# Last cross attention of a decoder: which key tiles GpSimd adds, and behind which step it splits the next keys

## The chip, the cores and the metric

One core of a Trainium2 chip runs the whole kernel. The metric is the device time of one execution in microseconds. The kernel before took 2197.64 us, the median of three runs (2193.97 to 2198.96).

## The reference, cut to what matters

The program is a decoder of two layers on x (4 sequences of 256 rows, width 128) with a context of 4 x 1601 rows of width 64. Layer 0: complex attention, self attention plus cross attention, an expert layer with Sinkhorn routing. Layer 1: attention with rotary and Fourier terms, a block with a self attention and a cross attention, an expert layer. The change is in the cross attention of that last block (`a2`), which has 16 heads of width 32:

```
q = einsum('bsc,hcd->bhsd', xn, wq)
k = einsum('btc,hcd->bhtd', yn, wk)
v = einsum('btc,hcd->bhtd', yn, wv)
a = softmax(einsum('bhsd,bhtd->bhst', q, k) * D ** -0.5, axis=-1)
o = einsum('bhst,bhtd->bhsd', a, v)
```

with s over 256 queries and t over 1601 keys. The softmax subtracts each query's largest score and divides by the sum over all 1601 keys.

## The kernel before, in words

`stage_cross` (L1907) does this attention in NS = 16 groups s, one for each of four batches and four quarters of the heads; G = 4 heads stand in a group. The keys of a head are 13 tiles t of 128 (the last has 65), and a group takes them two at a time in STEPS = 7 steps p; step 6 has the last tile alone. Every engine runs its own list of instructions in order, written out by loops over (s, p); semaphores tie them together.

A group has two passes over the scores. The first finds the largest score of each query. TensorE multiplies bf16 parts of queries and keys (L2002, 32 matmuls of 401 columns for group s + 1, spread over the steps of group s by MAX_AT), VectorE takes maxima from PSUM (L2120), joins them (L2123) and writes them negated in two bf16 parts (L2128, L2131); TensorE turns these around into a row (L2023), in step 6. The keys for that pass come in three blocks of 32 rows in `kb`: the high bf16 part, the low part, the high part again. GpSimd splits the float32 keys `k32` of a group into `kh` (L2198, cast) and `kl` (L2200, subtraction); this is `halves(s + 2)`, called in group s. SyncE copies them into `kb` with twelve DMAs of 100 KB (L2246): four wait for the cast, eight for the subtraction. The first score matmul of group s + 2 stands in step 0 of group s + 1, behind that step's transposed scores, and waits for all twelve and for twelve copies of queries (L2239).

The second pass makes transposed scores tile by tile (L2038 and L2042 into PSUM banks 2 to 5), ScalarE takes the exponential of both tiles of a step at once (L2146) into `prob`, one of three buffers, and TensorE multiplies it with the values (`values`, L2055). The denominators are sums over the keys, made by matmuls with a matrix of ones (`ones`). For a step p in ADDED, GpSimd first adds the step's two tiles (`add`, L2215) into one of two buffers `both` (they are tiles with other names, `yT` and `z`, in the profile), and TensorE needs one set of 4 matmuls on the sum (L2076), done one step later. For a step not in ADDED, TensorE runs one set for each tile (L2069), without GpSimd. A float32 matmul is two instructions in the profile, so L2076 has 8 a sum and L2069 16 a step of two tiles.

In a step p TensorE does, in this order: transposed scores of p, three scores for the maxima, `values` of p - 1, the rest of the step's scores (in step 6 the shift matmul L2023), `ones` of p - 1, and then key or value matmuls of later groups. In even groups these are the keys of groups s + 2 and s + 3 in steps 0 to 3 (taken from PSUM by ScalarE, L2157), in odd groups the values. So `halves(s + 2)` waits in even groups for the last key chunk, made at the end of step 3; in odd groups its keys have been there since the group before.

GpSimd's list in a group is: add of step p where p is in ADDED, the division of the last group in step 1 (L2206), and `halves(s + 2)` behind the add of step 2. Before, ADDED = (0, 1, 2, 4, 5). `add` waits for the step's exponential and for TensorE to have read the buffer two sums back. The exponential waits for the add three steps back, whose `prob` buffer it overwrites.

Of the kernel before, what the change touches and what calls it, by code (L numbers as in the profile page):

```python
# [1809 lines left out]

STEPS = 7
MAX_AT = ((0, 5), (5, 10), (10, 15), (15, 20), (20, 26), (26, 32), (32, 32))
ADDED = (0, 1, 2, 4, 5)
CHUNKS = ((0, 401), (401, 400), (801, 400), (1201, 400))


# [90 lines left out]
def stage_cross(nc, k, name, scale, cT, wk, wv, srcT, wq, q, qh, ql, both, out):  # L1907


    NS = B * 4  # L1910
# [13 lines left out]
    def tiles_of(p):  # L1924
        return [t for t in (2 * p, 2 * p + 1) if t < KT_CTX]

    def sums_made(s, p):

        return s * len(ADDED) + sum(a <= p for a in ADDED)

    def batch(s):
        return s // 8 + 2 * (s % 2)

    def part(s):
        return s // 2 % 4
# [7 lines left out]
    with ExitStack() as ctx:  # L1943
# [21 lines left out]
        with nc.Block() as block:  # L1965
            @block.gpsimd
            def _(g_):
                g_.memset(negm[:, :, :, :], 0.0)
                g_.memset(onesb[:, :], 1.0)
# [5 lines left out]
        with nc.Block() as block:  # L1975
            @block.tensor
            def _(pe):
# [68 lines left out]
                def values(s, p):  # L2046
# [5 lines left out]
                    for t in tiles_of(p):  # L2052
                        rows = tile_rows(t)
                        for g in range(G):
                            ins = pe.matmul(k.ps[32 * g:32 * g + 32, 6, 0:N], vs[0:rows, s % 3, t, 32 * g:32 * g + 32],  # L2055
                                            prob[0:rows, n % 3, g, (t % 2) * N:(t % 2 + 1) * N],
                                            start=(t == 0), stop=(t == KT_CTX - 1), skip_group_check=True)
                    if p in ADDED and p - 1 not in ADDED:
                        ins.then_inc(probs_used.s, 1)

                def ones(s, p):
                    n = s * STEPS + p
                    if p in ADDED and p - 1 not in ADDED:
                        return
                    if p not in ADDED:
                        for t in tiles_of(p):
                            rows = tile_rows(t)
                            for g in range(G):
                                ins = pe.matmul(k.ps[32 * g:32 * g + 32, 6, N:2 * N], k.ones[0:rows, 0:32],  # L2069
                                                prob[0:rows, n % 3, g, (t % 2) * N:(t % 2 + 1) * N],  # L2070
                                                start=False, stop=(t == KT_CTX - 1), skip_group_check=True)
                    if p - 1 in ADDED:
                        m = sums_made(s, p - 1)
# [118 lines left out]
            @block.gpsimd  # L2192
            def _(g_):
                def halves(s):
                    g_.wait_ge(taken.s, taken.at(turns.made_at["key", s, 3] + 1))
                    if s > 0:
                        g_.wait_ge(ops[(s - 1) % 2].s, ops[(s - 1) % 2].at(16 * NDMA * ((s - 1) // 2 + 1)))
                    g_.tensor_copy(kh[:, :], k32[:, s % 4, :]).then_inc(split.s, 1)  # L2198
                    g_.wait_ge(split.s, split.at(2 * s + 1))
                    g_.tensor_tensor(kl[:, :], k32[:, s % 4, :], kh[:, :], ALU.subtract).then_inc(split.s, 1)  # L2200

                def divide(s):
                    g_.wait_ge(inverted.s, inverted.at(s + 1))
                    g_.wait_ge(out_read.s, out_read.at(s + 1))
                    o = (batch(s) * 4 + part(s)) * N
                    g_.tensor_tensor(out[:, o:o + N], sums[:, s % 2, 0:N], inv[:, s % 2, :],  # L2206
                                     ALU.mult).then_inc(divided.s, 1)

                def add(s, p):
                    n, m = s * STEPS + p, sums_made(s, p)  # L2210
                    g_.wait_ge(exp_done.s, exp_done.at(n + 1))
                    if m > 2:
                        older, at = divmod(m - 3, len(ADDED))
                        g_.wait_ge(probs_used.s, probs_used.at(older * STEPS + ADDED[at] + 2))
                    g_.tensor_tensor(both[m % 2].rearrange("p (g n) -> p g n", g=G), prob[:, n % 3, :, 0:N], prob[:, n % 3, :, N:2 * N],  # L2215
                                     ALU.add).then_inc(added.s, 1)

                for s in range(-2, NS):
                    for p in range(STEPS):
                        if s >= 0 and p in ADDED:  # L2220
                            add(s, p)
                        if p == 1 and s > 0:
                            divide(s - 1)
                        if p == 2 and s + 2 < NS:
                            halves(s + 2)
                divide(NS - 1)

# [860 lines left out]
```

## Time and profile before

| | |
|---|---|
| median of three runs | 2197.64 us |
| the profiled execution | 2193.25 us, span 2191.1 us |
| mean granted TensorE clock | 0.888 |
| TensorE busy in the span | 1736.3 us, 79% |
| VectorE, ScalarE, GpSimd busy | 1170.5, 960.0, 524.3 us |
| the stage in question | about 1478 to 1977 us of the span |
| transposed scores L2038 in it | 133.6 us of TensorE |
| denominators L2069, L2076 in it | 27.3 and 2 x 25.0 us of TensorE |
| adds L2215 on GpSimd | 2 x 94.2 us |

The profile shows one execution. Busy time of an engine that is not the last to arrive costs nothing, so the shares only say where to look; the timelines say who waits for whom. A line of a timeline has a start in us from the span's start, a length in us, an engine, and in square brackets how long the engine had been idle and what ended that. SPq is SyncE's queue of DMA issues; such a line lasts as long as the issue, not as the transfer. PEld is a weight load.

### The profile page before, as it was taken

The page shows a single profiled execution, that of the slowest core. Times are in us where ns is not written, and L with a number is a line of the kernel's source. Part 1 is how long each engine was busy: PE and PEld are TensorE (multiplying, and loading weights), DVE is VectorE, ACT ScalarE, POOL GpSimd, SP SyncE. Part 2 cuts the span into 40 slices and gives each one's busy share as a digit, 9 for nine tenths or more (in the row PEclk, how much of TensorE's full clock was granted, in tenths as well). Part 3 has the DMA queues.
Part 4 walks back from the last instruction along what each step waited for, and adds up shares of the span by engine and source line. Part 5 has one row for each costly group of instructions (what it writes and reads, how often), then busy time and mean ns, then how long its engine had stood idle before and what let it go on. Part 6 is the DMA issues. An engine that isn't in the chain of part 4 may idle for free. (4 is left out here: it accounts for less than half of the span.)

```text
span 2191.1 us, 43006 instructions
## 1 busy us (share of the span) xinstructions
PE 1736.3 (79%) x16607; PEld 952.5 (43%) x16607; DVE 1170.5 (53%) x2374; ACT 960.0 (44%) x1576; POOL 524.3 (24%) x392
## 2 busy tenths in 40 slices
PE   3684485899997259989899588469999999995698
PEld 1452352233334236654456255324444444444465
DVE  2573487888881336449542466355555555542312
ACT  1351253699994213211354235225555555552133
POOL 2011413000000000007444000115555555542000
PEclk8796697899999579989999779769999999998699
DMA  8423321222200220100000000031221122100000
GB/s 220 125 71 111 103 61 49 55 49 48 50 19 8 94 73 30 44 1 0 1 1 1 1 2 17 5 92 35 49 52 38 45 54 52 41 13 1 29 29 29
DMA packets 113050, 98.58 MB, mean 45 GB/s; under 512 B 21825, under 2 KB 97257, under 8 KB 112361
## 3 DMA queue, kind: packets, MB, share of 16 engines
q1 hardware_dynamic: 112872, 96.13, 16.6%
q8 instruction: 122, 2.00, 0.4%
q14 instruction: 56, 0.45, 0.1%
HBM read 54.44 MB, written 21.96 MB: 35 GB/s over the span
## 5 line engine op out<-in xcount | busy, mean ns | idle before, releaser
L2120 DVE TENSOR_REDUCE ta_mxp<-ps 128x1 f32<-128x401 f32 x512 | 262.2, 568 | 222.8 <-PE ps L2002 216.5
L1152 DVE TENSOR_REDUCE ac_mxp<-ps 128x2 f32<-128x802 f32 x256 | 241.3, 989 | 40.9 <-PE ps L1070 39.9
L2146 ACT ACTIVATE ta_prob<-ps 128x2048 f32<-128x2048 f32 (+1 forms) x112 | 196.5, 1755 | 127.2 <-PE ps L2042 127.2
L1181 ACT ACTIVATE cT<-ps 128x512 f32<-128x512 f32 (+1 forms) x416 | 225.9, 596 | 29.7 <-PE ps L1095 20.8
L2002 PE MATMUL ps<-ta_kb,ta_qb 96*128 96x401 bf16 x512 | 131.9, 352 | 11.2 <-DMA ta_qb<-qxl 11.2
L2038 PE MATMUL ps<-qxf,ta_k 32*128 32x256 f32 (+1 forms) x1664 | 133.6, 405 | 6.3 <-ACT ta_prob L2146 3.6
L1109 PE MATMUL ps<-cT 128*32 128x256 f32 (+1 forms) x1664 | 134.3, 394 | 0.5 <-ACT cT L1181 0.5
L2612 PE MATMUL ps<-xT,e_wi 128*128 128x512 f32 x256 | 116.0, 612 | 15.1 <-DMA e_wd<-in_e_down 10.3
L2215 POOL TENSOR_TENSOR yT<-ta_prob 128x1024 f32<-128x1024 f32 x40 | 94.2, 2354 | 115.1 <-ACT ta_prob L2146 94.4
L2622 PEld LDWEIGHTS ps<-e_wd,e_hid 128*128 128x128 f32 x1024 | 116.9, 192 | 7.7 <-issue 7.7
L2215 POOL TENSOR_TENSOR z<-ta_prob 128x1024 f32<-128x1024 f32 x40 | 94.2, 2355 | 103.9 <-ACT ta_prob L2146 83.6
L2622 PE MATMUL ps<-e_wd,e_hid 128*128 128x128 f32 x1024 | 116.9, 275 | 0.0
L2055 PE MATMUL ps<-ta_prob,ta_vs 128*32 128x256 f32 (+1 forms) x1664 | 113.0, 385 | 0.0
L1070 PE MATMUL ps<-ac_kb,ac_qz 50*128 50x401 bf16 x512 | 88.5, 352 | 25.5 <-DMA ac_qb<-qc 18.2
L2684 DVE SCALAR_TENSOR_TENSOR x<-ps,weight,x 128x128 f32<-128x128 f32 x128 | 36.0, 344 | 133.2 <-PE ps L2622 133.2
L2645 ACT ACTIVATE e_gate<-ps 128x512 f32<-128x512 f32 x64 | 38.2, 597 | 133.3 <-PE ps L2612 133.3
L1095 PE MATMUL ps<-ac_qb,ac_kb 50*128 50x256 bf16 (+1 forms) x832 | 83.0, 275 | 13.1 <-ACT cT L1181 7.5
L1339 POOL TENSOR_TENSOR o<-o,fenc 128x512 f32<-128x512 f32 x32 | 40.2, 1267 | 214.8 <-DVE o L1326 214.7
L2038 PEld LDWEIGHTS ps<-qxf,ta_k 32*128 32x128 f32 (+1 forms) x1664 | 65.8, 183 | 56.6 <-issue 38.1
L2002 PEld LDWEIGHTS ps<-ta_kb,ta_qb 96*128 96x128 bf16 x512 | 36.8, 98 | 106.7 <-DVE ta_mxp L2120 59.5
L2648 ACT ACTIVATE e_hid<-ps,e_b 128x512 f32<-128x512 f32 x64 | 44.0, 687 | 89.3 <-PE ps L2612 88.0
L2612 PEld LDWEIGHTS ps<-xT,e_wi 128*128 128x128 f32 x256 | 47.5, 196 | 77.8 <-issue 38.1
(323 smaller groups left out, 3343.6 us busy)
## 6 DMA issues: line engine op xcount, KB each, us to landing
ta_kb<-ta_kh SPq DMA_DIRECT2D x128, 100.1 KB
ac_kb<-kc SPq DMA_DIRECT2D x192, 50.0 KB
ta_kb<-ta_kl SPq DMA_DIRECT2D x64, 100.1 KB
v<-p_vt SPq DMA_DIRECT2D x16, 256.0 KB, 3.2
a_vs<-v SPq DMA_DIRECT2D x32, 128.0 KB, 2.6
e_wi<-in_e_in SPq DMA_DIRECT2D x8, 512.0 KB, 3.5
e_wd<-in_e_down SPq DMA_DIRECT2D x16, 256.0 KB, 3.7
kc<-c_part SPq DMA_DIRECT2D x12, 300.0 KB, 3.0
```

The costliest lines, as they stand in the source:

```text
L1070: ins = pe.matmul(k.ps[:, i % 2 * 2 + h, 0:401], qz[r, s % NBUF, gg, qt * P:(qt + 1) * P], kb[r, s % NBUF, gg, c * 400:c * 400 + 401], sta ...
L1109: ins = pe.matmul(k.ps[32 * g:32 * g + 32, 6, 0:N], vs[0:rows, s % 2, t, 32 * g:32 * g + 32], prob[0:rows, n % 3, g % 2, g // 2 * N:(g // ...
L1152: v.tensor_reduce(mxp[:, qt * G + 2 * gg:qt * G + 2 * gg + 2, c:c + 1], k.ps[:, i % 2 * 2:i % 2 * 2 + 2, 0:401], AX.X, ALU.max).then_inc(s ...
L1181: a.activation(prob[0:rows, n % 3, h, :], k.ps[0:rows, bank(("part", n, h)), :], ACT.Exp, scale=scale).then_inc(exp_done.s, 1)
L2002: pe.matmul(bank[:, 0:401], qb[:, s % 2, g, qt * P:(qt + 1) * P], kb[:, s % 2, g, c * 400:c * 400 + 401], start=True, stop=True).then_inc( ...
L2038: pe.matmul(k.ps[0:rows, 2 + g, (t % 2) * N:(t % 2 + 1) * N], k32[r, s % 4, t * P:t * P + rows], q[r, part(s), cols], start=True, stop=False)
L2055: ins = pe.matmul(k.ps[32 * g:32 * g + 32, 6, 0:N], vs[0:rows, s % 3, t, 32 * g:32 * g + 32], prob[0:rows, n % 3, g, (t % 2) * N:(t % 2 + ...
L2120: v.tensor_reduce(mxp[:, qt * G + g, c:c + 1], k.ps[:, turns.bank(slot), 0:401], AX.X, ALU.max).then_inc(scores_read.s, 1)
L2146: a.activation(prob[0:rows, n % 3, :, 0:w], k.ps[0:rows, 2:6, 0:w], ACT.Exp, scale=scale).then_inc(exp_done.s, 1)
L2215: g_.tensor_tensor(both[m % 2].rearrange("p (g n) -> p g n", g=G), prob[:, n % 3, :, 0:N], prob[:, n % 3, :, N:2 * N], ALU.add).then_inc(a ...
L2612: ins = pe.matmul(k.ps[:, 2 * n + u % 2, :], wi[:, par, n * F + f * P:n * F + (f + 1) * P], rhs, start=True, stop=True)
L2622: ins = pe.matmul(k.ps[:, 4 + c, t * P:(t + 1) * P], hid[:, f, (c * 4 + t) * P:(c * 4 + t + 1) * P], wd[:, par, f * C:(f + 1) * C], start= ...
```

## The change

Step 3 joins the steps whose two key tiles GpSimd adds, so that only step 6, which has one tile, is left out. The call that splits keys moves from behind the add of step 2 to behind the add of step 3. All loops that depend on ADDED follow: GpSimd has six adds a group instead of five; `ones` of step 3 has no L2069 matmuls and keeps the L2076 set for step 2's sum; `ones` of step 4, which had nothing to do, has the L2076 set for step 3's sum.

```diff
@@ -1810,7 +1810,7 @@
-ADDED = (0, 1, 2, 4, 5)
+ADDED = (0, 1, 2, 3, 4, 5)
@@ -2221,7 +2221,7 @@
                             add(s, p)
                         if p == 1 and s > 0:
                             divide(s - 1)
-                        if p == 2 and s + 2 < NS:
+                        if p == 3 and s + 2 < NS:
                             halves(s + 2)
                 divide(NS - 1)
```

## Rows read from the trace of the kernel before

**Rows 1.** Windows, 50 us of the stage: busy time of each engine, clock, DMA share.
```profile
core 0: us, PE busy (x) PEld busy (x) DVE busy (x) ACT busy (x) POOL busy (x), PEclk, DMA share, GB/s
...
1650.00:1700.00 50.00, 48.38 (x631) 22.45 (x634) 27.88 (x56) 27.23 (x29) 28.12 (x15) 1.00 0.19 43
```

**Rows 2.** Timeline of TensorE in group s = 5.
```profile
1653.34 0.64 PE L2076 MATMUL ps<-z,ones 128*32 128x256 f32 x8
...
1658.45 0.64 PE L2076 MATMUL ps<-yT,ones 128*32 128x256 f32 x8
...
1659.11 0.44 PE L2015 MATMUL ps<-wc,cT 64*65 64x128 f32 x4
...
1663.03 1.07 PE L2069 MATMUL ps<-ta_prob,ones 128*32 128x256 f32 x16
...
1664.46 0.71 PE L2038 MATMUL ps<-qxf,ta_k 32*128 32x256 f32 x8
...
1670.61 0.30 PE L2023 MATMUL ps<-identb,ta_negm 128*32 128x128 bf16 x8 [0.82 <-DVE ta_negm L2131]
```

**Rows 3.** Timeline of the last group, s = 15, between steps 4 and 5.
```profile
1969.45 2.35 POOL L2215 TENSOR_TENSOR yT<-ta_prob 128x1024 f32<-128x1024 f32 x1 [4.32 <-ACT ta_prob L2146]
1969.68 0.71 PE L2038 MATMUL ps<-qxf,ta_k 32*128 32x256 f32 x8
```

**Rows 4.** Groups by line: busy us, mean ns of one, idle before.
```profile
L2215 POOL TENSOR_TENSOR z<-ta_prob 128x1024 f32<-128x1024 f32 x40 | 94.2, 2355 | 103.9 <-ACT ta_prob L2146 83.6 <-PE ps L2076 20.4
...
L2069 PE MATMUL ps<-ta_prob,ones 128*32 128x256 f32 (+1 forms) x384 | 27.3, 386 | 0.0
L2076 PE MATMUL ps<-z,ones 128*32 128x256 f32 x320 | 25.0, 384 | 0.0
```

**Rows 5.** Timeline of GpSimd in group s = 5: add, then split.
```profile
1654.15 2.35 POOL L2215 TENSOR_TENSOR z<-ta_prob 128x1024 f32<-128x1024 f32 x1 [2.92 <-PE ps L2076]
1656.45 1.52 POOL L2198 CAST ta_kh<-ta_k 128x1601 bf16<-128x1601 f32 x1
1658.05 3.02 POOL L2200 TENSOR_TENSOR ta_kl<-ta_k,ta_kh 128x1601 bf16<-128x1601 f32 x1
```

**Rows 6.** Timeline of group s = 6: the block of step 3, then GpSimd.
```profile
1689.60 0.64 PE L2076 MATMUL ps<-z,ones 128*32 128x256 f32 x8
...
1691.77 1.52 POOL L2198 CAST ta_kh<-ta_k 128x1601 bf16<-128x1601 f32 x1 [3.90 <-ACT ta_k L2157]
...
1693.37 3.23 POOL L2200 TENSOR_TENSOR ta_kl<-ta_k,ta_kh 128x1601 bf16<-128x1601 f32 x1
...
1699.48 2.36 POOL L2215 TENSOR_TENSOR yT<-ta_prob 128x1024 f32<-128x1024 f32 x1 [0.56 <-ACT ta_prob L2146]
```

**Rows 7.** Waits of SyncE in the stage: us in total, times, longest.
```profile
SPq L2263 <- DMA ta_kb<-ta_kh: 1.6, 1, 1.6
```

**Rows 8.** Timeline of SyncE: last four key copies issued in s = 0, 1, 6.
```profile
1508.98 2.50 SPq L2246 DMA_DIRECT2D ta_kb<-ta_kh  x4
...
1536.62 3.68 SPq L2246 DMA_DIRECT2D ta_kb<-ta_kh  x4
...
1700.21 2.50 SPq L2246 DMA_DIRECT2D ta_kb<-ta_kh  x4
```

**Rows 9.** Timeline of TensorE: first scores on the keys of rows 8.
```profile
1514.04 0.69 PE L2002 MATMUL ps<-ta_kb,ta_qb 96*128 96x401 bf16 x3
...
1545.85 0.69 PE L2002 MATMUL ps<-ta_kb,ta_qb 96*128 96x401 bf16 x3
...
1704.48 0.67 PE L2002 MATMUL ps<-ta_kb,ta_qb 96*128 96x401 bf16 x3
```

**Rows 10.** L2128 of all groups (ns min/median/max), and its timeline in s = 6.
```profile
L2128 DVE SCALAR_TENSOR_TENSOR ta_negm<-ta_mx x16: 193/673/675, 1476.6 to 1950.8; 128x8 bf16<-128x8 f32 x16
...
1701.22 0.67 DVE L2128 SCALAR_TENSOR_TENSOR ta_negm<-ta_mx 128x8 bf16<-128x8 f32 x1
```

## The prediction

> **What bounds the kernel now.** I read the page first, then the windows of the last cross attention, its groups by line, the timelines of TensorE, GpSimd and SyncE through two of its sixteen groups (s = 5 and s = 6), and last the waits of SyncE. A group s is seven steps p; s = 0 to 13 also prepare keys for group s + 2.
>
> In the stage TensorE is busy 48.4 of 50 us at granted clock 1.00, VectorE 27.9, ScalarE 27.2, GpSimd 28.1 [rows 1]. So TensorE's instruction stream sets the pace, except for one idle place a group: before the shift matmuls of step 6 (L2023) it waits 0.82 us for VectorE's negated maxima [rows 2]. In the last group, which has no maxima left, ScalarE's exponentials set the pace instead [rows 3]. Three things lie close behind. GpSimd adds a pair of key tiles in 2.35 us [rows 4], and splits keys in 1.52 + 3.02 us [rows 5]. SyncE then copies the split keys in twelve DMAs, which the first score matmul of the next group needs. And VectorE's maxima chain has one instruction (L2128) that overlaps a GpSimd add.
>
> **What the change removes and adds on TensorE.** Before, step 3's denominators are 16 L2069 instructions, followed by the 8 of L2076 for step 2's sum. This block runs from 1663.03 to the next L2038 at 1664.46, so 1.43 us. A block of 8 L2076 alone takes from 1658.45 to 1659.11, 0.66 us [rows 2]. After, step 4 holds 8 L2076 (gain 1.43 - 0.66 = 0.77), and step 5, which had no such block, holds 8 (loss 0.66, at its end). By count of instructions, with a group's busy time over its count as the price: 256 fewer of L2069 at 27.3 / 384 = 71 ns are 18.2 us, 128 more of L2076 at 25.0 / 320 = 78 ns cost 10.0 [rows 4], 8.2 us for the stage. The two readings differ because of what follows: step 5's maxima are computed before its new block, so VectorE's chain starts 0.77 earlier, and the 0.66 falls into the 0.82 us for which TensorE now waits at L2023. If nothing else moved, each group with maxima would gain about 0.75 us: 15 such groups, 11.3 us. In the last group the exponential of step 4 is done at about 1969.43 (the add that waits for it starts at 1969.45) and TensorE comes at 1969.68, so 0.25 us is gained; the new block of step 5 hides under the next exponential. Ceiling: 11.5 us.
>
> **What it adds on GpSimd.** One add more a group, 2.35 us, in front of the split. It waits for two things: step 3's exponential, and the buffer that the denominators of step 2's block have read. Such an add starts 0.81 us after that block's start (1653.34 there, add at 1654.15; the block of step 3 is at 1658.45) and the cast after it 2.30 us after the add's start [rows 2, 5].
> Odd s (5): the cast would start at 1658.45 + 0.81 + 2.30 = 1661.56 instead of 1656.45, 5.1 us later.
> Even s (6): there the split already waits for the last key chunk until 1691.77; now 1689.60 + 0.81 + 2.30 = 1692.71, 0.95 us later [rows 6].
> The added wait blocks what is queued behind it on GpSimd: cast, subtraction, the adds of steps 4 and 5. Add 4 would end at about 1668.6 (odd) and 1699.9 (even). The block that needs it is in step 6, behind L2023 (1670.6 before), so there are 1 us and more to spare; the exponentials need adds three steps back, which is not near.
>
> **Where the split keys are needed.** SyncE waits for the cast (4 DMAs), then the subtraction (8 DMAs). When its last issue has ended the data isn't there yet: at the end of the stage SyncE itself waits 1.6 us from its last key issue to its landing [rows 7]. So a group's first score can start 1.65 us after the last key issue ended. (The Trainium skill, Perfetto Trace Analysis, section DMA Instruction — HWDGE, says that the record of the issue doesn't contain the movement; the trace agrees with its 1.6 us.)
> Even s: last issue ends at 1511.48 (s = 0) and 1702.71 (s = 6), ready 1513.13 and 1704.36; needed 1514.04 and 1704.48 [rows 8, 9]. That is 0.91 and 0.12 us of slack; over the seven even groups 0.9 on average, and 0.12 is the smallest.
> Odd s: 1540.30 (s = 1), ready 1541.95, needed 1545.85: 3.9 us; over the seven odd groups 4.3.
> The copies move with the split, so they cost 5.1 - 4.3 = +0.8 us per odd group, and 0.95 - 0.9 = +0.05 per even group (up to +0.8 in s = 6). None of the 0.75 gain is left in either, because the wait is counted from GpSimd's chain and not from TensorE's. TensorE stands at the score matmul in order, so values, denominators and the next scores queue behind it.
> Bounds of the copies: eight issues of 0.6 us and the landing, 6.5 us after the subtraction, when none is held up; many groups have one long issue (4 issues took 3.68 instead of 2.50 [rows 8]). The average of before is kept. Without long issues the slack needed shrinks by about 0.6 us per group (odd +0.2, even -0.5); if every group had one, +0.5.
>
> **The maxima chain.** L2128 reads two SBUF operands. It takes 0.67 us in 15 of 16 groups and 0.19 in the first, where GpSimd has nothing to do [rows 10]. In group 6 it runs 1701.22 to 1701.89, and the GpSimd add of step 5 from 1699.48 to 1701.84: it ends 0.05 us behind the add. I take it as held until that add ends. After the change adds 4 and 5 run back to back behind the split. Subtraction's end in even groups 1696.61 + 0.95 = 1697.56, plus 4.70: add 5 ends at 1702.26, 0.4 later than before (0.2 where the subtraction took 3.02 and not 3.23). In odd groups 1661.07 + 5.1 + 4.70 = 1670.9 against 1670.18, 0.7 later (0.9 with the longer subtraction). The next group's first score moves by the same, 0.2 to 0.4 and 0.7 to 0.9 us later.
> The Trainium skill says this as a rule (SBUF — State Buffer, section Who interferes with whom): a VectorE instruction with two SBUF inputs and a GpSimd instruction that reads SBUF exclude each other, the later one waits for all of the other. The rows agree so far, but they show no case in which the add ends at another distance; were the 0.67 a fixed price of overlap, this term would be nothing.
> Both delays end at the same matmul, so the larger counts: odd groups +0.9, even groups +0.4.
>
> **Sum.** 7 x 0.9 + 7 x 0.4 = 9.1; group 14 has no split and gains 0.75, group 15 gains 0.25. In all 9.1 - 1.0 = 8.1 us slower. The profiled execution took 2193.25 us (span 2191.1), 4.4 under the median of 2197.64; on it the sum gives 2201.3, on the median 2205.7. I forecast 2205.8.
>
> **Rivals.**
> 1. Copies only: L2128 isn't held longer. 7 x 0.8 + 7 x 0.05 - 1.0 = +5.0, 2202.6. For it: 0.67 us is the same in 15 groups. Against: its end follows the add's end.
> 2. Copies land in their shortest time, and L2128 slips in between adds 4 and 5 (in odd groups it is ready 0.0 to 0.2 us after add 4's end, a close thing). 7 x 0.2 - 7 x 0.5 - 1.0 = -3.1, with half of it +0; centre 2196.5, no change.
> 3. The other side: neither copies nor lock are late, and TensorE keeps 0.75 us in 15 groups: -11.5, 2186.1. It decides if the copies need under 5.7 us from the subtraction's end; none of before did, as eight issues alone take 4.9. Or the data comes before my 1.65 us says. Against: the slack of 0.12 us in group 6.
> 4. The delays add up, since the lock shifts the start of a group and long issues fall more often into the later copies: odd +1.7, even +0.7, 16.8 - 1.0 = +15.8, 2213.4.
>
> **How the numbers follow.** Forecast 0.40, rival 1 0.20, rival 2 0.15, rival 3 0.10, rival 4 0.15. No change is within 0.2% (4.4 us), about what a measurement of this kernel tells. Slower: forecast, rival 4 and most of rival 1, 0.71; same: rival 2 and a rest of rival 1, 0.18; faster: 0.11. The range leaves out rival 3 and the upper half of rival 4: 2196 to 2213. The likeliest case's own range is 2202 to 2210.
>
> **What would show it.** In the profile after: L2069 has 128 instructions in the stage, L2076 768, and L2215 96 adds. The cast in odd groups starts about 5.1 us later against step 3's block, in even groups 0.95. The first score of each of groups 1 to 14 has an idle time ahead of it ended by a DMA of ta_kb, up to about 1 us; or L2128 grows to about 1.5 to 2.2 us, with a longer wait at L2023. From the first score at 1514.04 to that at 1704.48 are six groups, 63.5 us for two of them [rows 9]; after, two take 64.8. Step 4 is 0.77 shorter and step 5 0.66 longer. I am wrong if the first scores wait for nothing and L2023's wait shrinks, or if two groups take under 63.5 us.

## The result, and the profile after

| | before | after |
|---|---|---|
| median | 2195.99 us (4 runs) | 2210.97 us (2210.13 to 2213.12, 4 runs) |
| ratio to before | | 1.0067, 95% interval 1.0053 to 1.0080 |
| profiled execution | 2193.25 us | 2211.78 us |
| its span, mean granted clock | 2191.1 us, 0.888 | 2209.7 us, 0.879 |

The kernel became slower by 15.0 us; 8.1 were forecast. The time lies within the stated range (2196 to 2213), but just outside the likeliest case's own 2202 to 2210. One execution among all runs, of **after_copies_first** below, took 2662.78 us at a granted clock of 0.625, and as it is the one that was profiled, that run is read by its other times alone.

The counts of the changed kernel's stage are as forecast (groups by line):

```profile
L2215 POOL TENSOR_TENSOR yT<-ta_prob 128x1024 f32<-128x1024 f32 x48 | 113.1, 2356 | 133.8 <-ACT ta_prob L2146 91.0 <-PE ps L2076 42.8
...
L2076 PE MATMUL ps<-z,ones 128*32 128x256 f32 x384 | 30.7, 392 | 0.0
...
L2128 DVE SCALAR_TENSOR_TENSOR ta_negm<-ta_mx 128x8 bf16<-128x8 f32 x15 | 29.7, 1979 | 0.5
...
L2069 PE MATMUL ps<-ta_prob,ones 65*32 65x256 f32 x128 | 10.6, 405 | 0.0
```

The third line is the finding: L2128 takes 1.98 us on average instead of 0.67 [rows 10]. The timeline of group s = 5 of the changed kernel, steps 4 to 6:

```profile
1666.73 0.71 PE L2038 MATMUL ps<-qxf,ta_k 32*128 32x256 f32 x8
...
1670.86 0.71 PE L2038 MATMUL ps<-qxf,ta_k 32*128 32x256 f32 x8
...
1673.39 2.36 POOL L2215 TENSOR_TENSOR yT<-ta_prob 128x1024 f32<-128x1024 f32 x1
...
1674.98 0.66 PE L2038 MATMUL ps<-qxf,ta_k 32*65 32x256 f32 x8
...
1675.70 2.35 POOL L2215 TENSOR_TENSOR z<-ta_prob 128x1024 f32<-128x1024 f32 x1
...
1675.96 2.15 DVE L2128 SCALAR_TENSOR_TENSOR ta_negm<-ta_mx 128x8 bf16<-128x8 f32 x1
1678.14 0.19 DVE L2131 SCALAR_TENSOR_TENSOR ta_negm<-ta_mx,ta_negm 128x8 bf16<-128x8 f32 x1
...
1678.49 0.30 PE L2023 MATMUL ps<-identb,ta_negm 128*32 128x128 bf16 x8 [1.73 <-DVE ta_negm L2131]
```

Each L2038 opens a step. Step 4 takes 4.13 us (4.99 before), step 5 4.12 (3.56 before). Adds 4 and 5 run back to back behind the split. L2128 starts 0.26 us after add 5 and ends at 1678.11, 0.06 behind it. TensorE idles 1.73 us before L2023, against 0.82 [rows 2].

The waits of TensorE in the changed stage, 1500 to 1970 us (us in total, times, longest):

```profile
PE ps L2023 <- DVE ta_negm L2131: 22.1, 14, 2.0
...
PE ps L2002 <- DMA ta_kb<-ta_kh: 0.9, 4, 0.3
```

In that window the first was 12.3 us before, 15 times, 0.8 at most. The second says that the key copies ended the wait of only 4 first scores, by 0.9 us together.

What comes next in that group is the other part. Windows of the changed kernel, before, at and after this idle time (the column after POOL is the granted clock):

```profile
1643.00:1676.00 33.00, 30.98 (x432) 15.56 (x432) 19.49 (x39) 17.52 (x20) 19.77 (x11) 1.00 0.21 48
1676.00:1679.70 3.70, 1.83 (x38) 0.84 (x34) 2.31 (x2) 1.20 (x2) 2.06 (x1) 1.00 0.69 161
1679.70:1689.90 10.20, 10.20 (x77) 4.18 (x73) 2.60 (x5) 3.74 (x6) 2.35 (x1) 0.50 0.09 22
1689.90:1700.00 10.10, 9.49 (x114) 4.03 (x107) 5.20 (x10) 5.55 (x6) 5.04 (x3) 1.00 0.01 2
```

TensorE is busy for 1.83 of 3.70 us, and then the clock stands at its lower level (1.2 GHz) for 10.2 us, with the engine busy throughout. The group that begins there, s = 6, took 36.6 us from its first L2038 to the next group's, about 4.5 more than its like. It happens a second time at 1747.9, for 3.4 us, behind a wait of 1.96 us at L2023 (s = 7), and costs about 1.4: 0.2 at the end of s = 7 and 1.2 in s = 8 (33.00 us, 31.80 in s = 4). Not each such wait brings a fall: s = 3 and 11 wait 1.95 us at the same place, and none followed. Before, the clock stayed at its upper level from 1487.2 us, within group 0, to the end of the last group.

Where the profiled difference of 18.5 us stands, by the starts of the same instructions in both traces: 5.2 us had come up before the stage (first L2038 at 1483.31 instead of 1478.10), in code the change doesn't touch, where the clock fell at other places; 13.3 us come in the stage; nothing after it. Of the 13.3, the two clock falls are some 5.9, the groups' own time some 7.4. The 5.2 us ahead of the stage are of these two executions: in the traces of all kernels here that ran at the usual clock, whose code ahead of the stage is the same, it starts anywhere from 1476.3 to 1484.2.

### The profile page after: what moved, and what is told of

Read it like the earlier page. It is cut to its first block and busy times, and to the rows that moved or that the text cites. A ratio compares the mean times of both kernels' runs of the same rounds, so it can differ in the third digit from the quotient of the medians.

```text
span 2209.7 us, 42782 instructions
## 1 busy us (share of the span) xinstructions
PE 1745.0 (79%) x16479; PEld 955.2 (43%) x16479; DVE 1191.6 (54%) x2374; ACT 960.2 (43%) x1576; POOL 560.9 (25%) x408
## 3 DMA queue, kind: packets, MB, share of 16 engines
q8 instruction: 121, 1.98, 0.4%
## 5 line engine op out<-in xcount | busy, mean ns | idle before, releaser
L2215 POOL TENSOR_TENSOR yT<-ta_prob 128x1024 f32<-128x1024 f32 x48 | 113.1, 2356 | 133.8 <-ACT ta_prob L2146 91.0
L2038 PE MATMUL ps<-qxf,ta_k 32*128 32x256 f32 (+1 forms) x1664 | 136.2, 411 | 6.2 <-ACT ta_prob L2146 3.7
L2215 POOL TENSOR_TENSOR z<-ta_prob 128x1024 f32<-128x1024 f32 x48 | 112.7, 2349 | 89.5 <-ACT ta_prob L2146 48.9
L2038 PEld LDWEIGHTS ps<-qxf,ta_k 32*128 32x128 f32 (+1 forms) x1664 | 67.0, 186 | 61.4 <-issue 43.0
L1044 POOL TENSOR_TENSOR oc<-ac_sums,ac_inv 128x256 f32<-128x256 f32 x16 | 11.7, 728 | 291.9 <-ACT ac_inv L1194 291.9
```

The source lines that it names most:

```text
L2038: pe.matmul(k.ps[0:rows, 2 + g, (t % 2) * N:(t % 2 + 1) * N], k32[r, s % 4, t * P:t * P + rows], q[r, part(s), cols], start=True, stop=False)
```

## Experiments

Times are medians, ratios are to the kernel before, timed on the same chip. The first four runs were timed on one chip, after_filled, max_in_psum_filled, odd_early_psum_copies and before_psum_copies on a second, and added_alone, after_copies_first and odd_only_psum_copies on a third; between these three sets the ratios are compared and not the times. A group's time is from its first L2038 (whatever its line is called there) to the next group's. Each edit stands on the kernel named in brackets; of an edit, the lines that matter are shown.

**max_in_psum** (on the kernel after) and **before_max_in_psum** (on the kernel before): the joined maxima go to eight unused columns of the last score's PSUM bank.

```diff
-                    v.tensor_reduce(mx[:, :], mxp[:, :, :], AX.X, ALU.max).then_inc(vec.s, 1)
+                    mx = k.ps[:, turns.bank(("max", s, 31)), 404:404 + 2 * G]
+                    v.tensor_reduce(mx, mxp[:, :, :], AX.X, ALU.max).then_inc(vec.s, 1)
...
-                    v.scalar_tensor_tensor(out=high, in0=mx[:, :], scalar=-2.0, in1=mx[:, :],
-                                           op0=ALU.mult, op1=ALU.add).then_inc(vec.s, 1)
+                    v.tensor_scalar(high, mx, -1.0, None, ALU.mult).then_inc(vec.s, 1)
...
-                    v.scalar_tensor_tensor(out=low, in0=mx[:, :], scalar=-1.0, in1=high,
+                    v.scalar_tensor_tensor(out=low, in0=mx, scalar=-1.0, in1=high,
```

> The changed kernel, with the joined maxima in PSUM, so that neither L2128 (now a negation of one operand) nor L2131 reads two SBUF operands. Theory 1 (the maxima chain is held by GpSimd's add of step 5): L2128 falls from 1.66 to 2.38 us to 0.2 though it still overlaps an add; step 6 of the groups loses 0.9 to 1.3 us, and part of it is taken by the key copies, which come next: the first scores now wait for a DMA. About 0.4 us a group, 6 us in all, and up to 5 more if the clock no longer falls inside the stage: 2200 to 2205. Theory 2 (the key copies alone set the groups' start, the long L2128 lies beside them): L2128 shrinks and nothing is gained, 2211. Theory 3 (0.48 us is a fixed price of overlap, not a lock): L2128 keeps a length over 0.6.

Measured: 2229.35 us, ratio 1.0138 (1.0115 to 1.0160). The time was missed by 24 us and more, the first half of the mechanism held. Timeline of its group 1, and its waits:

```profile
1550.64 2.38 POOL L2215 TENSOR_TENSOR z<-ta_prob 128x1024 f32<-128x1024 f32 x1
...
1550.89 0.20 DVE L2128 TENSOR_SCALAR ta_negm<-ps 128x8 bf16<-128x8 f32 x1
1551.12 0.19 DVE L2131 SCALAR_TENSOR_TENSOR ta_negm<-ps,ta_negm 128x8 bf16<-128x8 f32 x1
...
1551.50 0.29 PE L2022 MATMUL ps<-identb,ta_negm 128*32 128x128 bf16 x8
...
1555.19 0.68 PE L2001 MATMUL ps<-ta_kb,ta_qb 96*128 96x401 bf16 x3 [1.46 <-DMA ta_kb<-ta_kh]
```

```profile
PE ps L2001 <- DMA ta_kb<-ta_kh: 26.5, 14, 2.8
```

Both instructions take 0.2 us in the middle of a GpSimd add: the held time is gone. The changed opcode of L2128 isn't what did it: L2131 is the instruction it was, with one operand moved. Step 6 takes 2.43 us, where it took 3.9 to 4.8 in the changed kernel. Now all 14 first scores wait for the key copies, 26.5 us together, and the clock falls 11 times inside the stage, 74.9 us at its lower level. So the copies are the second limit, right behind the maxima chain, and idle time on TensorE costs more than its length: the full groups without a fall took 31.65 to 32.23 us, those with one 34.0 and more. This is the kernel that rival 1 had priced, with the copies alone, at 5.0 us over the kernel before; it came to 30 and more.

> The kernel before, with the joined maxima in PSUM. Theory 1: L2128 falls from 0.67 to 0.2 in 15 groups, the wait at L2023 from 0.82 to about 0.35, 0.48 us a group: 7 us faster than before, 2189. Theory 2: the wait at L2023 shrinks, but in the even groups the key copies, with their 0.9 us of slack, take over: some 5 us faster, 2191.

Measured: 2191.26 us, ratio 0.9976 (0.9961 to 0.9991). The two theories lay too close together to be told apart by the time, but only one first score waited for a copy (0.2 us); step 6 went from 3.44 to 2.96 us in each group.

**odd_split_early** (on the kernel after): the odd groups split behind step 2. **odd_early_max_in_psum**: the same with the maxima in PSUM.

```diff
-                        if p == 3 and s + 2 < NS:
+                        if p == (2 if s % 2 else 3) and s + 2 < NS:
```

> The changed kernel, but the odd groups split their keys behind the add of step 2, as before; the even groups behind that of step 3. Theory 1: in odd groups add 5 no longer queues behind the split, only behind TensorE's reading of its buffer at the end of step 5; L2128 ends some 0.1 us later than before the change, a group costs +0.14 instead of +0.8: 4.6 us less than the changed kernel, 2206, and up to 5 less again if the clock stays up. Theory 2 (copies): they leave at the old time in odd groups, so the same saving, but then the first scores of odd groups in the changed kernel must have waited for a DMA, which the trace shows in 4 places only.

Measured: 2198.09 us, ratio 1.0004 (0.9992 to 1.0016): no slower than before. Its group 5:

```profile
1666.31 0.64 PE L2076 MATMUL ps<-z,ones 128*32 128x256 f32 x8
...
1667.12 2.36 POOL L2215 TENSOR_TENSOR z<-ta_prob 128x1024 f32<-128x1024 f32 x1 [1.77 <-PE ps L2076]
...
1667.85 1.68 DVE L2128 SCALAR_TENSOR_TENSOR ta_negm<-ta_mx 128x8 bf16<-128x8 f32 x1
```

Add 5 here waits 1.77 us with GpSimd idle, for TensorE to read its buffer in the new block of step 5, and L2128 is held for it again. An odd group took 31.96 us, +0.15 over before, as expected (three took 0.3 more, with 0.2 to 0.3 us of it waiting for a copy); and no clock fall is left in the stage. The saving of 13 us in the medians is more than the 9.6 expected at most. In the traces the stage is 10.2 us shorter, 5.9 of it the clock's, so the steady part and the clock's part both lay in the odd groups' split; the rest is within the spread of what comes ahead of the stage.

> Both: odd groups split behind step 2, and the maxima chain free of the lock. Theory 1: odd groups and group 14 keep TensorE's gain, -0.7 us each, and the 0.48 of the lock of before; even groups are held by the key copies, -0.2. Together 7 us or more under the kernel before, 2189 or less. If the copies of the even groups cost more than that, 2193.

Measured: 2196.87 us, ratio 0.9997 (0.9982 to 1.0012): a miss. Even groups run in 30.35 us, and the next group's first score waits for their copies (10.0 us in 7 places), with four clock falls. One of the falls came behind an idle time of 1.1 us, while none came behind 1.95 us in the changed kernel's s = 3 and 11: the length of one idle time doesn't say whether the clock falls.

**after_filled** and **max_in_psum_filled**: matmuls without a reader ahead of a wait that stays. The edit of the first; the second puts three in front of the first score's wait.

```diff
+                        for _ in range(0 if s == 0 else 2 + (s + 1) % 2):
+                            pe.matmul(bank[:, 0:400], wk[half(s), part(s) * P:(part(s) + 1) * P],
+                                      cT[half(s), at_batch(s):at_batch(s) + 400], start=True, stop=True)
                         pe.wait_ge(negmax.s, negmax.at(s + 1))
```

> The changed kernel, with matmuls whose result nobody reads in front of the wait for the negated maxima in step 6 (two of 400 columns in even groups, three in odd ones, 0.47 us each, inside an idle time of 1.2 to 2.1 us). If part of the changed kernel's time is the granted clock that falls after these idle times: no fall inside the stage, some 3 to 5 us less, 2206 to 2208. If the falls are chance or don't matter: 2211 or a little more.

Measured: 2207.65 us, ratio 1.0049 (1.0029 to 1.0068). The trace has no clock fall in the stage; odd groups take 32.84 us and even ones 32.01, +1.0 and +0.35 over before. The added matmuls were priced too low: they are float32 and so two instructions each, two of them take 1.61 us and three 2.28, more than the waits that they stand in, and cost up to 0.4 us a group. The interval overlaps that of the change, so the median alone doesn't show the clock's share.

> max_in_psum with three such matmuls (1.4 us) in front of a group's first score, where that kernel waits 1.9 us on average for the key copies. Clock theory: the falls inside the stage (11 in its trace) go, the groups take 31.7 to 32.2 us as its undisturbed ones do, 2197 to 2201 instead of 2229. If the time of max_in_psum comes from the copies themselves being slower, it stays near 2229.

Measured: 2211.97 us, ratio 1.0066 (1.0046 to 1.0086). The three matmuls of group 2:

```profile
1543.62 2.28 PE L2000 MATMUL ps<-cT,wc 64*128 64x400 f32 x6
```

By the ratios, more work on TensorE made the kernel 16 us faster, and one clock fall is left of 11 (10.2 us at the lower level instead of 74.9). 14 times 2.3 us of added work are more than the 25 us of waiting that they replace, so the gain comes from the clock: this shows its share. The time stayed 11 us over what I expected: most groups took 32.6 to 32.8 us, since the filling takes 2.3 us and not the 1.4 that I had priced, and an undisturbed group waits 1.1 to 1.7.

**odd_early_psum_copies** (on odd_early_max_in_psum), **before_psum_copies**, **after_copies_first** (on the kernel after): eight of the twelve key copies issued before the subtraction's.

```diff
-                    for k_part, n, count in ((kh, 0, 1), (kl, 1, 2), (kh, 2, 2)):
+                    for k_part, n, count in ((kh, 0, 1), (kh, 2, 1), (kl, 1, 2)):
```

> odd_early_max_in_psum, with the second copy of the high key parts issued before the low part's, so that eight of twelve copies go out during the subtraction and only four stand behind it. Copies then land some 0.8 us earlier. If the copies are what ends the wait of the even groups (7 waits, 10.0 us in its trace) and with it what makes the clock fall: waits under 1 us, few falls, groups near 30.4 to 31 us, 2180 to 2186. If the queue of copies is bound by their data and not by their order: no gain, 2197.

Measured: 2189.83 us, ratio 0.9954 (0.9935 to 0.9973). By the ratios this is 9 us faster than odd_early_max_in_psum, but over the 2180 to 2186 expected: seven first scores still wait, 7.3 us in all, up to 1.3, and one clock fall is left of four.

> before_max_in_psum with the same order of copies. There only one first score waited for a DMA: under 1 us gained, 2190 to 2191. Were it faster by more, the copies would bound it in a way that the trace doesn't show.

Measured: 2187.93 us, ratio 0.9949 (0.9929 to 0.9968). The interval overlaps that of before_max_in_psum, and in the traces the stage is 0.6 us shorter, as expected.

> The changed kernel with the second copy of the high key parts issued before the low part's: all copies land some 0.8 us earlier, the maxima chain is as in the changed kernel. Lock theory: only what the first scores waited for (0.9 us in 4 places) can go, 2210, within noise of 2211. Copies theory: 0.8 us in each of 7 to 14 groups, 2200 to 2205.

Measured: 2212.58 us, ratio 1.0068 (1.0050 to 1.0087), the changed kernel's time. Earlier copies alone give nothing back, so they are not what makes the change slow.

**added_alone** (on the kernel before): only ADDED is changed.

> Half of the change: GpSimd adds the tiles of step 3 as well, but the split stays behind the add of step 2 in all groups. In odd groups this is odd_split_early: +0.14 us each. In even groups the split waits for the last key chunk with adds 3, 4 and 5 behind it; add 3 ends near the end of step 5, where TensorE wants it (up to 1 us late), add 5 would end 1.8 us later than before. Lock theory: even groups +0.3 (L2128 slips in between two adds) to +1.8, so 2198 to 2210, and in no case under the kernel before. If only the copies mattered, both kinds of group would have them as early as before, and the kernel would be some 8 us faster than before, 2189.

Measured: 2217.90 us, ratio 1.0106 (1.0080 to 1.0132), slower than the whole change and than I expected. Its group 2:

```profile
1579.01 2.38 POOL L2215 TENSOR_TENSOR yT<-ta_prob 128x1024 f32<-128x1024 f32 x1
...
1580.48 0.94 DVE L2128 SCALAR_TENSOR_TENSOR ta_negm<-ta_mx 128x8 bf16<-128x8 f32 x1
1581.33 2.35 POOL L2215 TENSOR_TENSOR z<-ta_prob 128x1024 f32<-128x1024 f32 x1
1581.46 2.27 DVE L2131 SCALAR_TENSOR_TENSOR ta_negm<-ta_mx,ta_negm 128x8 bf16<-128x8 f32 x1
...
1583.88 0.41 PE L2023 MATMUL ps<-identb,ta_negm 128*32 128x128 bf16 x8 [2.42 <-DVE ta_negm L2131]
```

L2128 does slip in between adds 4 and 5: it ends 0.05 behind add 4 (1581.37). It gains nothing, since L2131 also reads two SBUF operands and is held by add 5 until 1583.68. Step 6 took about 5.0 us in even groups, so these took 32.9 to 33.1 us, +1.3 to +1.5, within what was expected. What was not expected is the clock: it fell three times, behind three of the waits of 2.4 us at L2023, for 27.3 us together. The groups behind these waits (s = 1, 3 and 7) took 36.51, 33.00 and 37.90 us instead of 31.95, some 12 us in all.

**odd_only_psum_copies** (on before_psum_copies): step 3 added in odd groups only.

```diff
+    def added_in(s):
+        return (0, 1, 2, 3, 4, 5) if s % 2 else (0, 1, 2, 4, 5)
```

The rest of the edit makes the counts of sums and semaphores follow.

> Step 3's tiles added by GpSimd in odd groups only, split behind the add of step 2 in all, joined maxima in PSUM, copies of the high part first: the even groups are those of before_psum_copies (their copies leave early enough), the odd ones those of odd_early_psum_copies (their GpSimd has room). Odd groups then keep TensorE's 0.8 us: 7 x 0.8 = 5.6 us under before_psum_copies, 2182 to 2184. If the odd groups' gain is lost again in the first scores of the next group, 2188.

Measured: 2184.36 us, ratio 0.9945 (0.9924 to 0.9965), the lowest median. Its interval lies almost on that of before_psum_copies (0.9949), so the times don't show the 5.6 us expected between the two; the traces do, where the stage is 5.7 us shorter up to the last group. Odd groups take 30.51 us, even ones 31.19 (31.81 and 31.66 before). Its first scores wait for no copy, and at L2027, the shift matmul, the waits are:

```profile
PE ps L2027 <- DVE ta_negm L2136: 2.8, 8, 0.4
```

That is 0.4 us in the even groups alone. Against before_psum_copies the odd groups keep 0.83 us each: step 4 is 0.87 shorter, step 5 0.56 longer and step 6 0.53 shorter, 0.35 of it the wait that was left at the shift matmul.

## Why the prediction was right or wrong

**TensorE's part: right.** Forecast -0.77 in step 4 and +0.66 in step 5; measured -0.86 and +0.57. The 0.8 us a group exist: odd_only_psum_copies keeps 0.83, by its trace.

**GpSimd's order: right.** The cast of s = 5 starts 2.30 us behind add 3's start and 3.1 behind step 3's block, as worked out; adds 4 and 5 follow back to back.

**The maxima chain: right, and now shown.** The length of L2128 follows the distance to add 5's end: 1.66 to 2.38 us, always ending 0.05 to 0.06 behind it; with operands in PSUM it is 0.2 us under the same add. A fixed price of overlap (rival 1's ground) is ruled out. This is what the Trainium skill's rule says (SBUF — State Buffer, section Who interferes with whom). The second instruction under the same rule, L2131, I had overlooked; in the change it never met an add, in added_alone it cost most. The size was a little too high: where the subtraction is the short one (3.02 us), an odd group became 0.6 us longer and an even one 0.1, where it is the long one, 0.8 and 0.3; I had worked out 0.7 and 0.2, 0.9 and 0.4, and put the larger of each pair into the sum for all groups.

**The copies: mis-sized.** Forecast +0.8 in odd groups and +0.05 in even ones, side by side with the lock. They were late in 4 groups, by 0.9 us in all, and after_copies_first gave nothing. Counted with my 1.65 us from the last issue, they landed 0.1 to 0.8 us before they were needed where the clock stayed up, because the lock had already moved that point. The 1.65 us was itself short: three of the four first scores that did wait started 1.77 us behind the last issue, so the smallest slack of before, 0.12 us, was none. Remove the lock and they limit all 14 groups (max_in_psum). As the larger of two delays counted, the error did not enter the sum.

**The sum of the groups: right, in part by luck.** Two groups were to take 64.8 us. Four groups of the changed kernel without a clock fall run between these first scores:

```profile
1783.06 0.69 PE L2002 MATMUL ps<-ta_kb,ta_qb 96*128 96x401 bf16 x3
...
1912.89 0.67 PE L2002 MATMUL ps<-ta_kb,ta_qb 96*128 96x401 bf16 x3 [0.22 <-DMA ta_kb<-ta_kh]
```

129.8 us for four, 64.9 for two. Over all groups that the clock left alone, an odd one took 32.6 us on average and an even one 32.05, +0.8 and +0.4 against the +0.9 and +0.4 forecast. The luck: I took the even groups' +0.4 for the lock's, but the held chain gave 0.1 to 0.3, and waits for copies the rest.

**Groups 14 and 15: group 14 wrong.** "Group 14 has no split and gains 0.75" fails: it took 27.47 us instead of 27.33 (group 15 gained 0.26, as forecast). Add 5 now uses the buffer that add 3 filled, which TensorE reads only in the new block at the end of step 5, so the add starts 0.8 us behind that block whatever the split does, and holds L2128. The prediction checked this wait for add 3 and not for add 5. In even groups it coincides with the split's delay, so of the even groups' +0.4 the split is not the only cause: s = 4 and 12 became longer by the same 0.14 us as group 14, which has no split.

**The clock: missing.** No rival had it. In the profile some 5.9 us of the stage are the clock's, behind idle times of 1.7 to 2.0 us that the held chain made. That is all of what lies between the 8.1 forecast and the stage's 13.3 us; the groups' own 7.4 are close to the forecast. So the forecast's mechanism held, and the step that it lacks is what the longer wait at L2023 does to the clock: the prediction put that at nothing without saying so. Rival 4's number (2213.4) came nearest, by a sum of delays that the traces don't show. What remains between the stage's 13.3 and the medians' 15.0 is within the intervals; the 5.2 us ahead of the stage are within the spread of its start over all traces, and prove nothing about the change.

## What to carry to other kernels

When work is moved onto GpSimd, look at every VectorE instruction with two SBUF operands that can meet it, also a tiny one: on a chain it costs what is left of the GpSimd instruction (0.19 us became up to 2.38 here), and one operand in PSUM frees it (0.2 us under the same add). For a double-buffered hand-over count the buffer's reader for each use, the last as well as the added one. An idle place that grows on a full TensorE can cost twice, once by its length and once by the clock behind it, and a wait that is removed in one place can come back in the next.

## What I had not expected of the hardware

Adding 2.3 us of useless matmuls a group made max_in_psum 16 us faster by the ratios, because 10 of its 11 clock falls went. Both falls in the changed kernel's stage came right behind an idle time of TensorE in one piece (1.73 and 2.0 us), and lasted 10.2 and 3.4 us. An 8-column VectorE instruction of 0.19 us took up to 2.38 us under a GpSimd add.
